# Latent attention of a decoder kernel: the causal mask added by DVE in PSUM, outputs in two banks, queries in one

## What is computed

```
x = _layernorm(x + _L0_attn_ref(x, ...))      # windowed attention
x = _layernorm(x + _L0_xattn_ref(x, ...))     # attention over 1601 context rows
x = _layernorm(x + _L0_ffn_ref(x, ...))       # quantised feed-forward
x = _layernorm(x + _L1_attn_ref(x, ...))      # latent attention: the part that changes
x = _layernorm(x + _L1_xattn_ref(x, ...))     # linear attention
x = _layernorm(x + _L1_ffn_ref(x, ...))       # 8 experts, 2 per token
```

```
c = hidden_states @ Wkvc
k_nope, v = (c @ Wkdec), (c @ Wvdec)          # KV = 4 heads of 128
q, k = concat([q_nope, q_rope]), concat([k_nope, k_rope])
scores = jnp.einsum('bqhd,bkhd->bhqk', q, k) * scale
scores = jnp.where(causal[None, None], scores, jnp.finfo(scores.dtype).min)
attn = jax.nn.softmax(scores, axis=-1)
out = jnp.einsum('bhqk,bkhd->bqhd', attn, v_p).reshape(b, s, H * FULL)
return out @ Wo
```

## Time and profile before

| | us |
|---|---|
| three runs, median (lowest to highest) | 857.29 (846.56 to 861.53) |
| the profiled execution | 850.55 |
| its span from the first to the last instruction | 848.7 |
| busy in the span: PE, DVE, ACT, POOL | 707.8, 501.8, 443.5, 213.2 |
| latent attention, from the first pair's scores to the last output projection | about 408 to 609 |

### The profile page before, as it was taken

One profiled execution on the slowest core, in us unless ns is written; L12 is line 12 of the kernel. 1 busy time (PEld: TensorE's weight loads), 2 busy tenths in 40 slices (PEclk: granted clock), 3 DMA queues, 4 the chain that ended last, 5 costly groups with the idle time before them and its releaser, 6 DMA issues.

```text
span 848.7 us, 14217 instructions
## 1 busy us (share of the span) xinstructions
PE 707.8 (83%) x4980; PEld 594.5 (70%) x4985; DVE 501.8 (59%) x1110; ACT 443.5 (52%) x1138; POOL 213.2 (25%) x351
## 2 busy tenths in 40 slices
PE   5887879999999998677989999999777249999970
PEld 4665778989899886355778878787665237777750
DVE  2676764684866754786545444454247647776644
ACT  3987664384654753565656454554320046565632
POOL 2554400000100101163123232333202513333324
PEclk9997999999999999898989999999997569999995
DMA  8993002202202200500100000000290111111104
GB/s 311 371 322 72 2 1 75 81 1 79 78 1 84 73 1 24 225 1 13 63 1 1 1 2 1 1 2 1 79 429 25 63 51 44 44 43 50 50 31 148
DMA packets 32259, 62.49 MB, mean 74 GB/s; under 512 B 2724, under 2 KB 26984, under 8 KB 29896
## 3 DMA queue, kind: packets, MB, share of 16 engines
q1 hardware_dynamic: 30184, 56.48, 19.3%
q0 software_dynamic: 2016, 5.22, 1.8%
HBM read 46.24 MB, written 15.55 MB: 73 GB/s over the span
## 4 chain that ended last, share of the span: by engine, by line
PE 51%; DVE 15%; ACT 14%; DMA 9%; issue 5%; POOL 5%; SPq 1%; another core or an unknown queue 0%; POOLq 0%; ACTq 0%; DVEq 0%
PE banks L1642 30%; PE bank L1642 20%; ACT arena L708 4%; DMA ys<-arena 4%; DVE U_split L1136 3%; DMA arena<-xs 2%; ACT arena L939 2%; ACT U_split L727 2%; DMA arena<-in_w_qr 2%; POOL rstd L529 1%; DVE mx L1090 1%; POOL arena L632 1%; POOL xs L622 1%; DVE arena L1309 1%; ACT arena L746 1%
## 5 line engine op out<-in xcount | busy, mean ns | idle before, releaser
L1642 PE MATMUL banks<-U_split 128*128 128x256 f32 (+2 forms) x808 | 172.8, 339 | 4.1 <-DVE U_split L1209 2.1
L1642 PEld LDWEIGHTS banks<-U_split 128*128 128x128 f32 x808 | 121.1, 192 | 22.5 <-issue 6.7
L1642 PE MATMUL bank<-U_split 128*128 128x256 f32 (+1 forms) x864 | 116.1, 291 | 16.0 <-DVE U_split L1136 14.6
L1642 PEld LDWEIGHTS bank<-U_split 128*128 128x128 f32 x864 | 109.0, 195 | 20.4 <-issue 16.5
L727 ACT ACTIVATE U_split<-arena 128x1024 fp32r (+6 forms) x122 | 98.7, 835 | 28.3 <-DVE arena L1561 11.4
L1642 PE MATMUL banks<-arena 128*128 (+4 forms) x632 | 108.0, 374 | 3.3 <-DVE arena L1084 2.3
L1642 PE MATMUL banks<-cst,arena 128*128 128x128 f32 (+1 forms) x594 | 88.6, 281 | 25.3 <-DMA arena<-xs 19.6
L1642 PEld LDWEIGHTS banks<-cst,arena 128*128 128x128 f32 (+1 forms) x594 | 70.8, 144 | 41.3 <-issue 15.7
L939 ACT ACTIVATE arena<-banks,dmx 128x128 f32<-128x128 f32 (+1 forms) x128 | 52.4, 417 | 74.4 <-DVE dmx L1410 74.4
L526 POOL TENSOR_SCALAR rstd<-mv 128x1 f32<-128x1 f32 x48 | 14.0, 292 | 304.2 <-DVE mv L1068 281.3
L1642 PEld LDWEIGHTS banks<-arena 128*128 128x128 f32 (+2 forms) x632 | 77.0, 180 | 16.1 <-DVE arena L1084 3.6
(11 more groups left out here) (215 smaller groups left out, 1238.1 us busy)
## 6 DMA issues: line engine op xcount, KB each, us to landing
arena<-in_w_exp SPq DMA_DIRECT2D x8, 1536.0 KB, 14.1
xs<-arena SPq DMA_DIRECT2D x8, 1032.0 KB, 14.5
arena<-in_ctxT SPq DMA_DIRECT2D x4, 1601.0 KB, 7.5
arena<-in_ctx SPq DMA_DIRECT2D x4, 1536.0 KB
arena<-in_w_f SPq DMA_DIRECT2D x3, 1024.0 KB, 11.9
arena<-xs SPq DMA_DIRECT2D x23, 129.0 KB
w_x<-in_w_x SPq DMA_DIRECT2D x9, 256.0 KB, 7.6
arena<-in_w_oh SPq DMA_DIRECT2D x1, 2048.0 KB, 8.0
```

Of the source, the lines that this page charges most:

```text
L1642: return nc.tensor.matmul(o, w, x, start=start, stop=stop, **k)
```

## The change

PE no longer writes the mask. Before, a head's scores began with a bf16 product of the identity and a stored 128x384 bias, and the two score products were added onto it. Now the score products stand alone, and DVE adds the 128x128 triangle in place to columns 0 to 127 and 256 to 383 of the bank, for both heads of a pair, before any maximum is taken. The stored bias shrinks to 128x128.

`d_outputs(p - 4)` moves on DVE from the head of step p to behind the maxima of p. `d_values` uses banks 6 and 1 by turns and waits for the low part two pairs back, not one. Queries all use bank 0, so `d_query(p + 1)` waits for the copy of query p.

```diff
             def d_query(p):
                 dve.wait_ge(G["d_q"], p + 1)
-                v.tensor_copy(qe[:, p % 3, :, :], PS[1 - p % 2][:, :]...).then_inc(G["d_q_sb"], 1)
+                v.tensor_copy(qe[:, p % 3, :, :], PS[0][:, :]...).then_inc(G["d_q_sb"], 1)
...
             for p in range(NP + 1):
                 b, q = divmod(p, PAIRS)
-                if p >= 4:
-                    d_outputs(p - 4)
                 if p + 2 < PAIRS:
                     d_split_w(p + 2)
...
                 if p < NP:
+                    masked = []
                     for h in (2 * p, 2 * p + 1):
                         dve.wait_ge(G["d_s"], h + 1)
+                        own = PS[2 + h % 2][:, 0:4 * P].rearrange("p (c d k) -> p c d k", c=2, d=2)[:, :, 0, :]
+                        masked.append(step(v.tensor_tensor(own, own, cbias[:, :].unsqueeze(1).broadcast_to([P, TPB, P]), ALU.add)))
+                    for h in (2 * p, 2 * p + 1):
+                        dve.wait_ge(G["dve_step"], masked[h % 2])
                         bank = PS[2 + h % 2]
                         v.tensor_reduce(dmx[:, h % 8, 0:1], bank[:, 0:P], AX, ALU.max, negate=True)...
                         v.tensor_reduce(dmx[:, h % 8, 1:2], bank[:, P:3 * P], AX, ALU.max, negate=True)...
+                if p >= 4:
+                    d_outputs(p - 4)
                 if p > 0:
                     d_rinv(p - 1)
...
             def d_query(p):
                 b, q = divmod(p, PAIRS)
                 pe.wait_ge(G["xT_done"], B + b + 1)
-                if p == 0:
-                    pe.wait_ge(G["f_sig"], 2 * NT)
-                elif p == 1:
-                    pe.wait_ge(G["xT_done"], 2 * B)
-                else:
-                    pe.wait_ge(G["d_q_sb"], p - 1)
+                if p > 0:
+                    pe.wait_ge(G["d_q_sb"], p)
...
-                mm(o[:, 0:3 * P], ident16[:, :], cbias[:, :], stop=False)
-                mm(o[:, 0:P], q[:, 0:P], k[:, 0:P], start=False, stop=False)
-                mm(o[:, P:3 * P], q[:, P:S], k, start=False, stop=True).then_inc(G["d_s"], 1)
+                mm(o[:, 0:P], q[:, 0:P], k[:, 0:P])
+                mm(o[:, P:3 * P], q[:, P:S], k).then_inc(G["d_s"], 1)
...
                     pe.wait_ge(G["ln_var"], 3 * NT)
+                elif p == 1:
+                    pe.wait_ge(G["xT_done"], 2 * B)
                 else:
-                    pe.wait_ge(G["d_o_lo"], p)
+                    pe.wait_ge(G["d_o_lo"], p - 1)
                 for h in (2 * p, 2 * p + 1):
-                    o = PS[6][(h % 2) * LAT:(h % 2 + 1) * LAT, :]
+                    o = D_VALUES[p % 2][(h % 2) * LAT:(h % 2 + 1) * LAT, :]
```

## The result

The changed kernel took 869.57 us (median of four runs, 861.1 to 873.43), against 856.29 for the kernel before: a ratio of 1.0141, 95% interval 1.01 to 1.0183. That is 13.3 us more. A second group of runs gave 1.0108 (1.001 to 1.0207). The forecast was 870 us and +13.5.

A forecast was written before the change was run, and what follows sets the result against it. PE was taken to bound the kernel from pair 6, a chain through ACT and DVE before; +9.5 us at full clock and +4 for the clock gave +13.5, 871 on the median, forecast as 870 us, range 854 to 884.

The forecast's parts named there:

- plain pair: Pair of the latent attention where nothing is held up: 4.40 us, 0.33 us less than before.
- scores of pair 7 to the first projection: At pair 11 PE waits for pair 7's low part; projection starts 24.8 us after pair 7's scores start: +4.05 us.
- idle before keys: At pairs 13 and 21 PE waits about 2.0 us for ACT's copy of the first keys: +0.82 us each.
- idle behind pair 29: PE idle 3.1 us before the rows' transposes, since the reciprocals come later: +0.9 us.
- end of the last sequence: The last values need no longer wait, thanks to the second output bank: -1.0 us.
- clock, beyond the fall that was there before: About half of PE's new gaps bring a fall of the granted clock, some 1.5 us each: +4 us.
- the first exponential: At the start of pairs 0 to 5: late by 0.82 us plus some 0.3 for query 1's wait.
- six gaps: New PE idle times: five of 2.0 to 2.1 us at projections and second keys, one of 3.1 behind pair 29.
- rival A: Clock falls at all six gaps, 2.7 us each: +26 us, 883 us; chance 0.22 with the one bank's cost.
- the cover: Slack in a plain pair before late exponentials lengthen it: about 0.8 us.
- Rival B: Only PE time counts and the adds hide: 10.6 + 1.0 us gained, 846 us; chance 0.10.
- rival C: Waits come but smaller, by more overlap or slack kept in pairs 7 to 11: +2 to +5 us, 861; chance 0.18.

The follow-up runs named there:

- the keys apart: Kernel before with only the keys' order changed: second key products at q = 6, rows' transposes at q = 7; 844.16 us against 853.18, ratio 0.99.

## Why the prediction was right, step by step

| step | predicted | measured |
|---|---|---|
| exponentials after the start of the scores | 2.50 | 2.50 |
| cost of two adds, by starts | 0.68 | 0.67 |
| plain pair | 4.40 | 4.39 |
| pairs 1 to 5, sum of the longer periods | 3.4 | 3.3 |
| exponentials of pair 7 to 10 | 17.7 | 17.7 |
| scores of pair 7 to the first projection | 24.8 | 24.9 |
| idle before keys | 2.0 | 1.90 |
| idle behind pair 29 | 3.1 | 2.98 |
| end of the last sequence | -1.0 | -1.2 |
| clock, beyond the fall that was there before | 4 | 4.4 |

The periods come from the first exponentials in the trace of after (421.40, 443.80, 459.43, 477.15); the scores of pair 7 start 2.50 us before 459.43, so that 481.82 is 24.9 behind them. The clock's price is read from the same places with and without a fall: pair 13 to 14 took 10.48 us against 8.90 for pair 21 to 22; pair 27 to 28 took 13.74 against 12.20; pair 29 to 30 took 9.31 against 8.00 in the second trace of the changed kernel. That is 1.6 + 1.5 + 1.3 = 4.4. Taken from the 12.9 us of the whole stretch it leaves 8.5, and with 1.1 for the first exponential 9.6 us at full clock, where the sum had 9.5.

That the clock's term fits as well is in part luck. It was half of six gaps at 1.5 us each, and no row of before had shown a short fall. The second trace of the changed kernel has falls at two of the six gaps; and with the low part ahead at q = 3, one fall behind the keys of pair 13 cost 3.05 us (11.95 against 8.90).

The first exponential is the one term that the profile of after can't tell. It came 4.7 us later than before, but the clock was already low from 395.4 to 412.5, in the feed-forward part and the first products of the stage. In the run with two sets of adds it was not: there the first key products were at 402.60 and the first exponential at 411.7, 9.1 us apart against 7.36 before (404.51 to 411.87); less one set (0.68) that is 1.06, for which I had 1.1.

The Trainium skill, page "TensorE: Matmul & The Clock Gate", section on the second failure mode, says that frequent short idles between groups of products make the clock fall and rise again. The traces agree in part. Of ten waits of 1.9 us in the two traces of the changed kernel four were followed by low clock, and one of the two of 3.0 us: not all six gaps, as in rival A.

The places differ more than the lengths do. In these two traces and those of the two kernels with the low part ahead, the 1.9 us wait before the second keys was followed by low clock in six of eight cases; the 1.9 us wait before the projections, which only the changed kernel has, in one of its six. No run shows why, and the sum took all gaps as alike.

Where the reasoning had a hole though the sum was right: the prediction said of the low part's move that it "saves nothing", which holds for pairs 0 to 5, and priced it at zero elsewhere. In fact a plain pair takes 0.64 us more without it, once the adds are there. My sum went by the changed order, in which the loop is open, and did not ask what the old order would have made of the adds. The same blind spot led to the wrong expectation for the low part ahead in all pairs. Two smaller terms were off without weight for the sum: the cover is 0.6 us and not 0.8, and DVE's added work from pair 11 on was counted for 24 pairs where there are about 20.

Rival B fell: PE's time was not all that counts. Of rival C nothing was seen. The single query bank cost nothing.

## What to carry to other kernels

Moving work from the busiest engine to one that is idle for 40% of the time can lose, if the receiving engine stands in a chain of single results: two adds of 0.43 us a pair cost about 2%, 18 us, here. Read for each step where its result is awaited and by whom, and split the loop into stretches with cover and without; the same edit gave 0.33 us a pair in the first and took 0.67 in the second, and doing it only in the first, together with the keys apart, beat both kernels. When an instruction moves behind others on an in-order engine, look for the one iteration in which another engine waits for it, and look too for a loop that it closed at its old place.

## What I had not expected of the hardware

A DVE add in place in PSUM, fp32 with a bf16 operand from SBUF, took 0.43 us for 256 columns, about the same as a two-input operation with an SBUF output (0.42), and the next instruction starts 0.34 us behind it. Where the next one waits for its end it starts 0.45 us behind (419.46 to 419.91 in the run with each head's maxima behind its own add), and splitting the pair of adds gained nothing in pairs 0 to 5.

The clock did not fall for the same 1.9 us wait at the same place in every execution. In this kernel a term for the clock could be given only as a chance and a price.
